# Local attention in a four-layer stream: softmax weights divided ahead of their transposes, values as the stationary operand

## Chip, cores and metric

One of the cores of a Trainium2 chip runs the whole program. The metric is the device time of one execution in microseconds (us), the lower the better. Engines are named as in the profile: PE is TensorE (PEld its weight loads), DVE VectorE, ACT ScalarE, POOL GpSimd, SP the engine that issues the DMAs.

## What is computed

The input is x, 4 sequences of 512 tokens by 128 features, float32. Four blocks follow each other, each added to x:

```python
x = x + attn_a(layernorm(x))      # softmax attention, 16 heads of 8
x = x + ffn(layernorm(x))         # two layers, below
x = x + attn_b(layernorm(x))      # linear attention, 16 heads of 8
x = x + ffn(layernorm(x))         # the same weights again
```

The change touches only the local attention in ffn. For each of its two layers:

```python
h = shift_token(x)                        # half of the features from the token before
q, k, v = split(h @ wqkv)                 # 8 heads of 64
q, k = l2norm(q) * qs, l2norm(k) * ks
q, k = rotary_xpos(q, k)
# windows of 64 queries; keys and values of this window and the one before
attn = softmax(where(mask, -max, 8 * q @ k.T))
x = x + (attn @ v) @ wo
h = layernorm(shift_token(x)) @ w1 + b1
x = x + (h_a * gelu(h_g)) @ w2 + b2
```

## The kernel before

A first part (until some 255 us) does attn_a for all sequences. Then comes one long stream, `stream`, in which the change lies. It works on 64 tiles of 128 tokens: 2 calls of ffn x 2 layers x 4 sequences x 4 tiles. Four tiles, one sequence in one layer, are a group; there are 16 groups. After the second layer of the first call each sequence also goes through attn_b, so 4 of the 16 groups carry that work too.

The order of work is written out by hand. `STEP` lists for each engine the stages in the order in which it does them in a step, each with a lag: stage s with lag l handles tile (step - l). Group stages (wo, center, var, w1, w2) act only at a group's last tile. `engine_plan` unrolls this. The engines then run on their own, in order, and meet by semaphores only.

One tile goes through these stages (lag in brackets):

- project (0): PE makes q, k, v in nine matmuls (L1253 to L1255), one PSUM bank each. ACT squares q and k (squares, L1462) and copies v to `V` (values, L1471). SP moves the values' halves to `VS` by two DMAs (L1148), so that each window finds its keys' values over 128 partitions.
- rope (0): DVE makes the rotation out of PSUM, four multiplications (L1615, L1619) and a reduction of the squares (L1626). POOL adds the two products (L1182) and scales by the norm (L1187), which ACT makes (norm, L1511).
- turn (1): PE transposes q and k (L1264, 8 transposes), ACT copies them to `QT` and `KT` (L1482, L1486).
- scores (1): PE adds the mask by matmuls (L1277) and multiplies queries and keys (L1292) into two banks, one for each half j of the heads. soften (1): DVE takes the maxima (L1651), ACT the exponentials into `PW` (L1496, 8 instructions).
- turn_p, turn_p_2 (2): PE transposes the weights of each half (L1302, 8 transposes). ACT copies the first half to `PT` (L1518), DVE the second (L1643).
- sums (2), last in the step: PE multiplies, with `PT` stationary and the values moving (L1313). The values have a 65th column of ones, so each result carries its denominator. DVE takes the reciprocal (L1658) and multiplies it in, to `ON` (L1662).
- turn_o (3): PE transposes `ON` (L1325, 4 transposes), ACT copies the result to `OT` (L1527).
- wo (3): PE multiplies `OT` by wo (L1350). center and var (4) are the layer norm's matmuls (L1368, L1374); DVE applies it (L1677, L1681). w1 (5) is L1381, w2 (6) is L1389. DVE adds w2's result in (L1714, L1718 in the first layer, three instructions; L1707 in the second, one).

The 8 banks of PSUM are dealt out in turn in the order of PE's plan. Each new use waits until the one eight uses before it has been read (`take` and `FREED`). So the order of PE's stages also sets which reader each stage waits for:

```python
def take(kind, i):
    x = at[kind, i]
    if x >= BANKS:
        earlier, j = order[x - BANKS]
        name, value = FREED[earlier]
```

`PW` and `PT` have four slots of one half each, `V` and `VS` four of a tile.

Of the kernel before, what the change touches and what calls it, by code (L numbers as in the profile page):

```python
# [14 lines left out]
P = 128  # L15
# [110 lines left out]
def build(nc, a, out):  # L126
    with ExitStack() as top:
# [46 lines left out]
        g.V = sb("V", [P, 4, HW, DW + 1])  # L174
# [39 lines left out]
        def weights_of_stream():  # L214

            todo = []
            for layer in range(LAYERS):
                def row(name):
                    return a[name][layer:layer + 1]

                by_head = row("L0_ffn_wo").rearrange("a (cc c j d) n -> c d (a cc) j n", cc=2, c=2, j=2)
                todo += [
                    *((g.wo[DW * c:DW * c + DW, layer, 2 * cc:2 * cc + 2, :], by_head[c, :, cc])
                      for c in range(2) for cc in range(2)),
# [85 lines left out]
def attention_a(nc, a, g):  # L310
# [69 lines left out]
    with ExitStack() as ctx:  # L380
# [38 lines left out]
        with block:  # L419
# [40 lines left out]
            def _(pool):  # L460
# [8 lines left out]
                nc.gpsimd.memset(g.V[:, :, :, DW:DW + 1], 1.0).then_inc(s("front_ones"), 1)  # L469
# [227 lines left out]
            def _(act):  # L697
                nc.scalar.preload_act_table_set(EXP_AND_LN)
                for work, i in plan:
# [83 lines left out]
                    elif work == "front":  # L783
# [7 lines left out]
                        act.wait_ge(s("front_ones"), 1)  # L791
                        nc.scalar.activation(g.V[:, i, :, 0:DW],
# [189 lines left out]
def of_first(k):  # L982
# [5 lines left out]
    "PE": [("latent", 8, of_sequence),  # L988
           ("project", 0, of_tile), ("features_b", 10, of_sequence), ("turn", 1, of_tile), ("features_a", 1, of_first), ("project_a", 2, of_first),
           ("context", 9, of_sequence),  # L990
           ("turn_o", 3, of_tile), ("project_b", 10, of_sequence), ("w1", 5, of_group), ("turn_p", 2, of_tile), ("turn_p_2", 2, of_tile),
# [3 lines left out]
           ("var_y", 10, of_sequence), ("w2", 6, of_group), ("wo", 3, of_group), ("sums", 2, of_tile), ("store", 6, of_end)],  # L995
    "ACT": [("latent", 8, of_sequence),
            ("squares", 0, of_tile), ("features_b", 10, of_sequence), ("turn", 1, of_tile), ("features_a", 1, of_first), ("values", 0, of_tile), ("turn_o", 3, of_tile),
            ("center_mlp", 4, of_group), ("center_a", 3, of_first), ("center_b", 7, of_sequence),
            ("center_y", 10, of_sequence), ("split", SEQS, of_tile), ("w1", 5, of_group), ("turn_p", 2, of_tile), ("keys_b", 8, of_sequence),
            ("norm", 0, of_tile), ("var_mlp", 4, of_group), ("var_a", 3, of_first), ("var_b", 7, of_sequence),  # L1000
            ("var_y", 10, of_sequence), ("soften", 1, of_tile), ("store", 6, of_end)],
    "DVE": [("lead", 0, of_lead), ("latent", 8, of_sequence), ("rope", 0, of_tile), ("project_a", 2, of_first), ("context", 9, of_sequence), ("project_b", 10, of_sequence),
            ("w1", 5, of_group), ("turn_p_2", 2, of_tile), ("keys_b", 8, of_sequence), ("soften", 1, of_tile),
            ("tokens_b", 9, of_sequence), ("var_mlp", 4, of_group), ("var_a", 3, of_first),
            ("var_b", 7, of_sequence), ("var_y", 10, of_sequence), ("wo", 3, of_group),
            ("w2", 6, of_group), ("sums", 2, of_tile)],
    "POOL": [("lead", 0, of_lead), ("split", SEQS, of_tile), ("scale", 0, of_tile), ("w2", 6, of_group),
             ("wo", 3, of_group), ("latent", 8, of_sequence), ("var_y", 10, of_sequence)],
    "SP": [("values", 0, of_tile), ("store", 6, of_end)],
# [31 lines left out]
def stream(nc, a, g, out):  # L1041
# [5 lines left out]
    for stage, i in engine_plan("PE"):  # L1047
# [4 lines left out]
        elif stage in ("scores", "sums", "keys_b", "tokens_b"):  # L1052
# [7 lines left out]
        elif stage[:7] == "center_":  # L1060
            order += [("center", number[stage[7:], i])]
        elif stage[:4] == "var_":
            order += [("var", number[stage[4:], i])]
        elif stage in ("turn_o", "wo", "w2", "context", "features_b", "project_b", "store", "features_a", "project_a"):
            order += [(stage, i)]
    at = {x: i for i, x in enumerate(order)}

    def bank(kind, i):
        return at[kind, i] % BANKS
# [5 lines left out]
             "scores": ("exped", lambda i: i + 1), "turn_p": (("p_copied", "p_copied_2"), lambda i: i // 2 + 1),  # L1075
             "sums": ("divided", lambda i: i + 1), "turn_o": ("o_copied", lambda i: i + 1),
# [721 lines left out]
```

## Time and profile before

| | |
|---|---|
| median of 3 runs | 1001.57 us (1001.5 to 1002.53) |
| the profiled execution | 1000.6 us, of which the span is 998.5 us |
| mean granted clock of TensorE | 0.996 of full speed |
| busy: PE, DVE, ACT, POOL | 94%, 73%, 73%, 39% |
| a plain group of the stream, and one with attn_b | 41.8 us, 54.3 us |

The span runs from the first to the last instruction on the core; the 2.1 us beside it are what the device's time has around it. A busy share is a mean over stages that differ. Durations in the rows are of single instructions, which overlap at their ends with their neighbours on the same engine; from start to start they are closer together.

### The profile page before, as it was taken

Reading aid. Unit: us, or ns where it says so; the run is one execution under the profiler, and the core shown is the slowest. Engines: PE = TensorE matmul, PEld = TensorE weight load, DVE = VectorE, ACT = ScalarE, POOL = GpSimd, SP = SyncE. Lnnn points to the kernel's source line nnn. Section 1 sums busy time; section 2 is a strip of 40 time slices with the busy share of each in tenths; the row PEclk is TensorE's granted clock in tenths of the full one; section 3 lists DMA queues with packets and bytes.
Section 4 is the critical chain, followed back from the end, with each engine's and each line's share of the span. In section 5 each row is a group of like instructions: output and inputs, shape, how many; then the busy total and the mean of one; then the engine's idle time right before and its main releaser. Section 6 shows DMA issues by size and latency. Waiting matters only on the chain.

```text
span 998.5 us, 22947 instructions
## 1 busy us (share of the span) xinstructions
PE 939.0 (94%) x8744; PEld 575.5 (58%) x8744; DVE 732.4 (73%) x1218; ACT 728.0 (73%) x1563; POOL 386.4 (39%) x272
## 2 busy tenths in 40 slices
PE   8999999999789999999999999999999999999985
PEld 4333333333566676666766566666666666766752
DVE  6887878886487777777777677777677777777741
ACT  3577777778688786877867677777778868788662
POOL 2110113123366536455443534434355454544411
PEclk9999999999999999999999999999999999999999
DMA  2210100000211101011000101000011011110100
GB/s 82 66 40 10 26 2 2 3 1 2 59 29 28 24 18 33 18 28 23 18 23 17 23 18 23 17 13 22 18 23 29 18 26 25 23 39 17 34 22 11
DMA packets 23303, 23.72 MB, mean 24 GB/s; under 512 B 8626, under 2 KB 15068, under 8 KB 23196
## 3 DMA queue, kind: packets, MB, share of 16 engines
q1 hardware_dynamic: 23196, 22.27, 9.3%
q8 instruction: 71, 1.16, 0.5%
q14 instruction: 36, 0.29, 0.1%
HBM read 6.16 MB, written 1.05 MB: 7 GB/s over the span
## 4 chain that ended last, share of the span: by engine, by line
PE 54%; DVE 10%; ACT 5%; issue 3%; POOL 1%; DVEq 0%; POOLq 0%; ACTq 0%
PE psum L1381 8%; PE psum L1350 6%; PE psum L1292 5%; PE psum L1389 4%; PE psum L1313 4%; PE psum L1302 3%; PE psum L1264 3%; PE psum L1253 3%; DVE BS L1619 3%; PE psum L1374 3%; PE psum L1255 3%; PE psum L1254 3%; DVE A L1615 3%; PE psum L1368 2%; PE psum L1277 2%
## 5 line engine op out<-in xcount | busy, mean ns | idle before, releaser
L1182 POOL TENSOR_TENSOR A<-A,BS 128x1024 f32<-128x1024 f32 x62 | 146.2, 2359 | 207.1 <-DVE BS L1619 206.9
L878 DVE TENSOR_REDUCE a_M<-psum 128x2 f32<-128x1024 f32 x128 | 155.3, 1220 | 34.0 <-PE psum L651 33.2
L1187 POOL TENSOR_TENSOR A<-A,RN 128x1024 f32<-128x1024 f32 x62 | 117.9, 1902 | 89.5 <-ACT RN L1511 86.0
L1496 ACT ACTIVATE f_PW<-psum,f_NM 128x128 f32<-128x128 f32 x512 | 138.5, 381 | 18.7 <-DVE f_NM L1651 18.7
L774 ACT ACTIVATE a_PT<-psum 128x1024 f32<-128x1024 f32 x128 | 128.8, 1020 | 23.2 <-PE psum L661 23.0
L1615 DVE TENSOR_TENSOR A<-psum,cos 128x512 f32<-128x512 f32 x124 | 84.8, 684 | 35.1 <-ACT SQ L1462 35.1
L1651 DVE TENSOR_REDUCE f_NM<-psum 128x4 f32<-128x512 f32 x128 | 82.1, 683 | 38.5 <-PE psum L1292 38.5
L1462 ACT ACTIVATE SQ<-psum 128x512 f32<-128x512 f32 x124 | 72.1, 624 | 49.4 <-PE psum L1255 46.4
L1381 PE MATMUL psum<-f_mid,w 128*128 128x512 f32 (+1 forms) x192 | 87.0, 603 | 2.7 <-DVE f_mid L1681 2.7
L1313 PEld LDWEIGHTS psum<-f_VS,f_PT 128*64 128x64 f32 x1024 | 64.5, 137 | 38.8 <-issue 38.3
L1619 DVE TENSOR_TENSOR BS<-psum,sin 128x512 f32<-128x512 f32 x124 | 84.2, 679 | 0.0
L572 PE MATMUL psum<-a_PT,a_VA 128*12 128x256 f32 x1024 | 79.6, 383 | 0.6 <-ACT a_PT L774 0.6
L1626 DVE TENSOR_REDUCE SS<-SQ 128x16 f32<-128x1024 f32 x62 | 74.8, 1207 | 0.0
L1313 PE MATMUL psum<-f_VS,f_PT 128*64 128x65 f32 x1024 | 73.5, 225 | 0.6 <-DVE f_PT L1643 0.4
L1313 PE MATMUL psum<-V,f_PT 128*64 128x65 f32 x1024 | 73.6, 225 | 0.0
L1264 PE MATMUL psum<-const,A 128*128 128x128 f32 x512 | 66.8, 274 | 5.7 <-POOL A L1187 3.7
L1264 PEld LDWEIGHTS psum<-const,A 128*128 128x128 f32 x512 | 59.6, 141 | 14.7 <-POOL A L1187 4.7
L1302 PE MATMUL psum<-const,f_PW 128*128 128x128 f32 x512 | 67.1, 273 | 1.0 <-DVE BS L1619 1.0
L1292 PE MATMUL psum<-f_KT,f_QT 64*64 64x128 f32 x2048 | 67.6, 270 | 0.4 <-ACT f_KT L1486 0.4
L1302 PEld LDWEIGHTS psum<-const,f_PW 128*128 128x128 f32 x512 | 58.5, 141 | 12.9 <-issue 12.9
L1313 PEld LDWEIGHTS psum<-V,f_PT 128*64 128x64 f32 x1024 | 64.5, 137 | 0.0
L1292 PEld LDWEIGHTS psum<-f_KT,f_QT 64*64 64x64 f32 x2048 | 61.2, 134 | 5.0 <-ACT f_KT L1486 0.9
(212 smaller groups left out, 1946.1 us busy)
## 6 DMA issues: line engine op xcount, KB each, us to landing
f_VS<-V SPq DMA_DIRECT2D x112, 130.0 KB, 2.3
raw<-L_ffn_wqkv_dram SPq DMA_DIRECT2D x2, 768.0 KB, 4.8
a_XT<-L_attn_a_x_dram SPq DMA_DIRECT2D x4, 256.0 KB, 2.9
out_dram<-f_OUT SPq DMA_DIRECT2D x4, 256.0 KB, 2.3
w<-L_ffn_w_dram SPq DMA_DIRECT2D x2, 341.0 KB
tables<-const_dram SPq DMA_DIRECT2D x1, 512.0 KB, 3.7
wo<-L_ffn_wo_dram SPq DMA_DIRECT2D x8, 64.0 KB
const<-const_dram SPq DMA_DIRECT2D x1, 264.0 KB, 3.1
```

Of the source, the lines that this page charges most:

```text
L774: nc.scalar.activation(PT[:, i % 4, :, :], psum[:, pair("by_key", i), :], ACT.Exp, scale=float(DA) ** -0.5).then_inc(s("exped"), 1)
L878: nc.vector.tensor_reduce(M[:, quads % 2, t, 2 * j:2 * j + 2], psum[:, pair("scores", i), :], AX_X, ALU.max).then_inc(s("maxed"), 1)
L1182: nc.gpsimd.tensor_tensor(A[:, k % 2, :, :], A[:, k % 2, :, :], BS[:, k % 2, :, :], ALU.add)\
L1187: nc.gpsimd.tensor_tensor(x, x, RN[:, k % 2, :, None].to_broadcast([P, 2 * HW, DW]), ALU.mult)\
L1264: last = nc.tensor.transpose(dst[:, P * c:P * c + P], A[:, k % 2, w, P * c:P * c + P], g.ident)
L1292: last = nc.tensor.matmul(dst[j][WIN * w:WIN * w + WIN, P * c:P * c + P].rearrange("p (s x) -> p s x", s=2), QT[rows, k % 2, c, WIN * w:WI ...
L1302: last = nc.tensor.transpose(dst[:, P * c:P * c + P], PW[:, u % 4, c, :], g.ident)
L1313: last = nc.tensor.matmul(dst[WIN * w:WIN * w + WIN, c, :], PT[:, u % 4, c, WIN * w:WIN * w + WIN], values[:, k % 4, 2 * c + j, :], start= ...
L1381: nc.tensor.matmul(take(kind, 3 * i + blk)[0:w, :], w1[:, layer, first + lo:first + lo + w], mid[:, :], start=True, stop=True).then_inc(s( ...
L1496: last = nc.scalar.activation(PW[:, u % 4, c, :], psum[:, bank("scores", u), P * c:P * c + P], ACT.Exp, bias=NM[:, u % 4, c:c + 1])
L1615: nc.vector.tensor_tensor(A[:, k % 2, w, :].rearrange("p (h d) -> p h d", d=DW), x.rearrange("p (h d) -> p h d", d=DW), g.cos[:, layer, t, ...
L1619: nc.vector.tensor_tensor(BS[:, k % 2, w, :].rearrange("p (h s d) -> p h s d", s=2, d=DW // 2), x.rearrange("p (h s d) -> p h s d", s=2, d ...
```

## The change

The softmax weights are divided by their sum before they are transposed, not the result after the multiplication:

- A new stage weigh, lag 2. DVE sums the exponentials of a tile over its keys (one reduction over 128 x 1024 of `PW`) and takes the reciprocal of the 8 sums. POOL multiplies `PW` by it in place.
- turn_p moves to lag 3, to the head of PE's and DVE's step. It waits for POOL's multiplication. Both copies to `PT` are DVE's, one behind the other, first in its step; ACT's is gone.
- sums moves to lag 3 on PE, from the end of the step to behind turn. The values (64 columns, no ones) are now the stationary operand and `PT` moves. The result is then already turned, features by tokens, and takes one bank for the tile, not two. ACT copies it to `OT`.
- turn_o, `ON`, the division and the column of ones go away. wo's rows stand in plain order and are loaded by one DMA a layer in place of four.
- Around it, project stands behind turn_p on PE, latent behind project. On DVE the layer norm's application and the addition of w2's result move from the end of a step to the head of the next, ahead of weigh and rope. On ACT values stands ahead of turn.

```diff
 STEP = {
+    "PE": [("turn_p", 3, of_tile), ("turn_p_2", 3, of_tile),
+           ("project", 0, of_tile), ("latent", 8, of_sequence), ("features_b", 10, of_sequence), ("turn", 1, of_tile),
+           ("sums", 3, of_tile), ("features_a", 1, of_first), ("project_a", 2, of_first), ("context", 9, of_sequence),
+           ("project_b", 10, of_sequence), ("w1", 5, of_group),
...
+           ("var_y", 10, of_sequence), ("w2", 6, of_group), ("wo", 3, of_group), ("store", 7, of_end)],
+    "ACT": [("squares", 0, of_tile), ("latent", 8, of_sequence), ("features_b", 10, of_sequence), ("values", 0, of_tile),
+            ("turn", 1, of_tile), ("sums", 3, of_tile), ("features_a", 1, of_first),
...
+    "DVE": [("lead", 0, of_lead), ("turn_p", 3, of_tile), ("var_mlp", 5, of_group), ("var_a", 4, of_first),
+            ("var_b", 8, of_sequence), ("var_y", 11, of_sequence), ("w2", 7, of_group),
+            ("weigh", 2, of_tile), ("latent", 8, of_sequence), ("rope", 0, of_tile),
+            ("project_a", 2, of_first), ("context", 9, of_sequence), ("project_b", 10, of_sequence),
+            ("w1", 5, of_group), ("keys_b", 8, of_sequence), ("soften", 1, of_tile),
+            ("tokens_b", 9, of_sequence), ("wo", 3, of_group)],
+    "POOL": [("lead", 0, of_lead), ("split", SEQS, of_tile), ("weigh", 2, of_tile), ("scale", 0, of_tile), ("w2", 6, of_group),
              ("wo", 3, of_group), ("latent", 8, of_sequence), ("var_y", 10, of_sequence)],
...
+                    elif stage == "weigh":
+                        k = i
+                        pool.wait_ge(s("den_recip"), k + 1)
+                        x = PW[:, 2 * (k % 2):2 * (k % 2) + 2, :, :].rearrange("p u c x -> p (u c) x")
+                        nc.gpsimd.tensor_tensor(x, x, RD[:, k % 2, :, None].to_broadcast([P, 2 * PAIRS, P]), ALU.mult)\
+                            .then_inc(s("weighed"), 1)
...
                 def turn_p(u):
-                    pe.wait_ge(s("exped"), u + 1)
+                    pe.wait_ge(s("weighed"), u // 2 + 1)
...
+                    dst = take("sums", k).rearrange("p (c x) -> p c x", c=PAIRS)
+                    pe.wait_ge(s("p_copied"), 2 * k + 2)
+                    for c in range(PAIRS):
+                        for w, values in ((0, VS), (1, V)):
+                            for j in range(2):
                                 last = nc.tensor.matmul(
-                                    dst[WIN * w:WIN * w + WIN, c, :], PT[:, u % 4, c, WIN * w:WIN * w + WIN],
-                                    values[:, k % 4, 2 * c + j, :], start=True, stop=True)
+                                    dst[DW * j:DW * j + DW, c, WIN * w:WIN * w + WIN],
+                                    values[:, k % 4, 2 * c + j, :],
+                                    PT[:, (2 * k + j) % 4, c, WIN * w:WIN * w + WIN], start=True, stop=True)
+                    last.then_inc(s("sums"), 1)
...
-                def turn_o(k):
...
+                    elif stage == "weigh":
+                        k = i
+                        dve.wait_ge(s("exped"), 2 * k + 2)
+                        if k >= 2:
+                            dve.wait_ge(s("weighed"), k - 1)
+                        x = PW[:, 2 * (k % 2):2 * (k % 2) + 2, :, :].rearrange("p u c x -> p (u c) x")
+                        nc.vector.tensor_reduce(RD[:, k % 2, :], x, AX_X, ALU.add).then_inc(s("den"), 1)
+                        dve.wait_ge(s("den"), k + 1)
+                        nc.vector.reciprocal(RD[:, k % 2, :], RD[:, k % 2, :]).then_inc(s("den_recip"), 1)
```

## Rows read from the trace of the kernel before

**Rows 1.** The page's first part: busy time, share, instructions of each engine.
```profile
PE 939.0 (94%) x8744; PEld 575.5 (58%) x8744; DVE 732.4 (73%) x1218; ACT 728.0 (73%) x1563; POOL 386.4 (39%) x272
```

**Rows 2.** Windows: stretch, length, busy time per engine, PEclk, DMA share, GB/s.
```profile
250.00:270.00 20.00, 14.64 (x174) 10.19 (x173) 7.80 (x15) 10.42 (x26) 7.76 (x8) 0.91 0.27 74
...
386.40:428.20 41.80, 40.74 (x420) 28.64 (x419) 32.28 (x58) 32.58 (x81) 20.69 (x14) 1.00 0.11 24
...
607.00:661.30 54.30, 51.72 (x461) 34.39 (x461) 39.70 (x74) 39.41 (x93) 23.16 (x16) 1.00 0.08 19
```

**Rows 3.** Waits of PE: us in total, times, longest us.
```profile
PE psum L1277 <- DVE BS L1619: 12.9, 20, 1.3
...
PE psum L1253 <- DVE f_mid L1677: 4.9, 4, 1.2
```

**Rows 4.** Timeline of PE, behind w1: start, length, instructions, [idle before].
```profile
455.63 1.03 PE L1264 MATMUL psum<-const,A 128*128 128x128 f32 x8
456.50 0.60 PE L1325 MATMUL psum<-const,f_ON 128*128 128x128 f32 x4
456.94 1.04 PE L1302 MATMUL psum<-const,f_PW 128*128 128x128 f32 x8
458.61 0.41 PE L1277 MATMUL psum<-constb 64*64 64x512 bf16 x4 [0.64 <-DVE BS L1619]
...
459.82 2.85 PE L1389 MATMUL psum<-f_hidden,w 128*128 128x512 f32 x6
462.60 0.27 PE L1313 MATMUL psum<-f_VS,f_PT 128*64 128x65 f32 x1
...
463.68 0.50 PE L1253 MATMUL psum<-f_qkv_h,HH 128*128 128x512 f32 x1
...
465.87 1.03 PE L1264 MATMUL psum<-const,A 128*128 128x128 f32 x8
```

**Rows 5.** Groups by line and shape: busy us, mean ns, idle before.
```profile
L1187 POOL TENSOR_TENSOR A<-A,RN 128x1024 f32<-128x1024 f32 x62 | 117.9, 1902 | 89.5 <-ACT RN L1511 86.0
...
L1626 DVE TENSOR_REDUCE SS<-SQ 128x16 f32<-128x1024 f32 x62 | 74.8, 1207 | 0.0
...
L1313 PE MATMUL psum<-f_VS,f_PT 128*64 128x65 f32 x1024 | 73.5, 225 | 0.6 <-DVE f_PT L1643 0.4 <-issue 0.2
...
L1662 DVE TENSOR_TENSOR f_ON<-psum,f_RD 128x256 f32<-128x256 f32 x128 | 54.3, 424 | 4.6 <-DVE f_RD L1658 0.2
...
L1643 DVE COPY f_PT<-psum 128x512 f32<-128x512 f32 x64 | 43.6, 682 | 4.0 <-PE psum L1302 2.1
...
L1658 DVE RECIPROCAL f_RD<-psum 128x4 f32<-128x4 f32 x128 | 22.1, 173 | 0.0
```

**Rows 6.** Instructions of L1681: min, median, max ns, starts.
```profile
L1681 DVE TENSOR_SCALAR f_mid<-f_mid,vecs x16: 485/487/985, 317.3 to 982.6; 128x512 f32<-128x512 f32 x16
```

**Rows 7.** Timeline of ACT behind w1.
```profile
453.22 2.17 ACT L1496 ACTIVATE f_PW<-psum,f_NM 128x128 f32<-128x128 f32 x8 [0.34 <-DVE f_NM L1651]
455.23 1.14 ACT L1462 ACTIVATE SQ<-psum 128x512 f32<-128x512 f32 x2
...
456.75 0.59 ACT L1486 ACTIVATE f_KT<-psum 128x512 f32<-128x512 f32 x1
```

**Rows 8.** Timeline of DVE, behind w1 and behind w2.
```profile
452.49 1.29 DVE L1651 TENSOR_REDUCE f_NM<-psum 128x4 f32<-128x512 f32 x2 [0.56 <-PE psum L1292]
...
455.98 0.69 DVE L1615 TENSOR_TENSOR A<-psum,cos 128x512 f32<-128x512 f32 x1 [1.10 <-ACT SQ L1462]
...
462.70 1.53 DVE L1714 SCALAR_TENSOR_TENSOR HH<-psum,vecs,Y 64x512 fp32r<-64x512 f32 x2 [1.32 <-PE psum L1389]
464.27 0.75 DVE L1718 SCALAR_TENSOR_TENSOR Y<-psum,vecs,Y 128x512 f32<-128x512 f32 x1
```

**Rows 9.** Timeline of POOL behind w1.
```profile
452.96 1.90 POOL L1187 TENSOR_TENSOR A<-A,RN 128x1024 f32<-128x1024 f32 x1 [3.50 <-ACT RN L1511]
```

More of the change, by code:

```diff
@@ L219, in row @@
                     return a[name][layer:layer + 1]
-                by_head = row("L0_ffn_wo").rearrange("a (cc c j d) n -> c d (a cc) j n", cc=2, c=2, j=2)
                 todo += [
-                    *((g.wo[DW * c:DW * c + DW, layer, 2 * cc:2 * cc + 2, :], by_head[c, :, cc])
-                      for c in range(2) for cc in range(2)),
+                    (g.wo[:, layer, :, :], row("L0_ffn_wo").rearrange("a (c p) n -> p (a c) n", p=P)),
                     (g.w1[:, layer, :], row("L0_ffn_w1").rearrange("a p n -> (a p) n")),
@@ L1000 @@
             ("norm", 0, of_tile), ("var_mlp", 4, of_group), ("var_a", 3, of_first), ("var_b", 7, of_sequence),
[L1001 to L1006, printed above, removed]
@@ L1051, in stream @@
             order += [("turned_q", i), ("turned_k", i)]
-        elif stage in ("scores", "sums", "keys_b", "tokens_b"):
+        elif stage in ("scores", "keys_b", "tokens_b"):
             order += [(stage, 2 * i), (stage, 2 * i + 1)]
@@ L1063, in stream @@
             order += [("var", number[stage[4:], i])]
-        elif stage in ("turn_o", "wo", "w2", "context", "features_b", "project_b", "store", "features_a", "project_a"):
+        elif stage in ("sums", "wo", "w2", "context", "features_b", "project_b", "store", "features_a", "project_a"):
             order += [(stage, i)]
@@ L1074, in stream @@
              "turned_q": ("qk_copied", lambda i: 2 * i + 1), "turned_k": ("qk_copied", lambda i: 2 * i + 2),
-             "scores": ("exped", lambda i: i + 1), "turn_p": (("p_copied", "p_copied_2"), lambda i: i // 2 + 1),
-             "sums": ("divided", lambda i: i + 1), "turn_o": ("o_copied", lambda i: i + 1),
+             "scores": ("exped", lambda i: i + 1), "turn_p": ("p_copied", lambda i: i + 1),
+             "sums": ("o_copied", lambda i: i + 1),
              "wo": ("y_mid", lambda i: i + 1), "center": ("ln_used", lambda i: i + 1),
@@ L1146, in _ @@
                         if k >= 4:
-                            sp.wait_ge(s("sums"), 2 * k - 6)
+                            sp.wait_ge(s("sums"), k - 3)
                         sp.dma_start(VS[WIN:P, k % 4, :, :], V[0:WIN, k % 4, :, :]).then_inc(s(f"moved{k % 4}"), 16)
@@ L1231, in take @@
                         name, value = FREED[earlier]
-                        if earlier == "turn_p":
-                            name = name[j % 2]
                         pe.wait_ge(s(name), value(j))
@@ L1342, in _ @@
                         sums(i)
-                    elif stage == "turn_o":
-                        turn_o(i)
                     elif stage == "wo":
@@ L1512, in _ @@
                           .then_inc(s("norm"), 1)
[L1513 to L1521 removed]
+                    elif stage == "sums":
                         k = i
                         m, t = k // TILES, k % TILES
[L1524 removed]
+                        act.wait_ge(s("sums"), k + 1)
                         if m >= 1:
@@ L1527, in _ @@
                         nc.scalar.activation(OT[:, :, P * t:P * t + P],
-                                             psum[:, bank("turn_o", k), :].rearrange("p (c x) -> p c x", c=PAIRS),
+                                             psum[:, bank("sums", k), :].rearrange("p (c x) -> p c x", c=PAIRS),
                                              ACT.Copy).then_inc(s("o_copied"), 1)
```

81 lines of the change are left out of this document (17 added, 64 removed).

## The prediction

> **What bounds the kernel now.** I read the busy shares first. PE is busy for 94% of the span, DVE for 73%, ACT for 73%, POOL for 39% [rows 1]. The page says that a busy PE is modelled, so the share alone proves nothing. Next came the windows of one group each. A plain group of four tiles (12 of the 16) takes 41.8 us, and PE is busy for 40.74 of them. A group with the work of attention b takes 54.3, PE 51.72 [rows 2]. In both DVE has room: 32.28 of 41.8, 39.70 of 54.3. Third, the waits of PE: the largest, over the whole span, is 12.9 us, in 20 waits, the mask matmul L1277 for a bank that the rotation on DVE (L1619) still reads [rows 3]. So in the stream TensorE's own issue rate sets the time, at a granted clock of 1.00, the 2.4 GHz level. A microsecond taken from PE there is a microsecond of the kernel, until another engine's chain becomes longer than PE's step.
>
> A rule of the Trainium skill speaks against this reading. "Perfetto Trace Analysis", section Identifying the Most-Contended Engine, says that matmul busy time is no measure of how near TensorE is to its roofline, and that the busy share of LDWEIGHTS is. That share is 58% here [rows 1], and 28.64 of 41.8 us in a plain group [rows 2]. Taken as the judge of what bounds, it would leave PE idle a third of the time. By that rule the removed transposes would come out of idle time, and the sum would be 0; by the rows, in which PE starts stage after stage with 0.64 us of waiting in a step [rows 4], it is what follows. I go by the rows and keep the other as a rival.
>
> **Part 1, PE: turn_o goes.** The four transposes of turn_o start at 456.50 and the next stage at 456.94: 0.44 us for a tile [rows 4]. 64 tiles x 0.44 = 28.2 us. Their records sum to more than that, since neighbours overlap; the distance from start to start is the price.
>
> **Part 2, PE: values stationary.** sums keeps its count of matmuls; the weights stay 128 x 64, the moving operand goes from 65 columns to 64. One tile's sums take 463.68 - 462.60 = 1.08 us, for 32 records of 225 ns [rows 4, 5], that is, they run two by two, on either half of the columns. In the old order consecutive matmuls went to output rows 0 to 63 and 64 to 127, by w; in the new order they do so by j. I take the overlap as kept. The gain is 1/65 of 1.08, 0.017 us, x 64 = 1.1 us. If the pairs no longer overlap, 32 records cost twice as much: 1.08 us more per tile, 69 us. That is one of the cases below, and the far bound.
>
> **Part 3, DVE.** It loses two reciprocals and two multiplications a tile: 2 x (173 + 424) = 1.19 us. It gains the second copy (682 ns), a reduction over 128 x 1024 in SBUF, whose nearest row is L1626 with the same shape (1207 ns), and one reciprocal of 8 columns, nearest the 173 ns of 4 columns [rows 5]. Added 2.06, net 0.87 us a tile, 3.5 a group: 35.8 us of DVE in a plain group, 43.2 in one with attention b. DVE stays below PE, but at nine tenths of a plain group of about 40 us. The reduction has bounds of 0.68 (half as wide, if it were like the maximum over 512 of rows 8) and 1.5 us; the upper one would add 0.3 x 4 = 1.2 us of DVE to a group.
>
> **Part 4, POOL and ACT.** POOL gets one multiplication of 128 x 1024 by a broadcast for each tile, nearest L1187 with 1902 ns [rows 5]: 7.6 us a group. The window's POOL time goes from 20.69 [rows 2] to 28.3 of 40, no bound. ACT loses its copy of the turned half and keeps the one of turn_o under another name. Neither costs anything by itself, because PE's 40 us cover both. The Trainium skill ("SBUF — State Buffer", in the part on reading the engine diagram) says that VectorE in a two-port mode and GpSimd lock each other out of a shared port for a whole instruction. By a lock held through one of POOL's 1.90 us instructions, each of the 16 L1681 would come up to 1.9 us late, 30 us in all if PE waited for each; the row that bears on it shows a median of 487 ns and a largest of 985 [rows 6], so 0.5 us at most so far, and w1 comes some 3 us behind it in PE's new order. I take nothing for it.
>
> **Part 5, waits: PE's own order.** The bank order changes with the stages. A step has ten banks, not twelve, and the mask matmuls now take the banks of turn_p, which the two first copies free early. The 12.9 us at L1277 go [rows 3]. What is late next, step by step:
>
> *The step behind w1.* Let M be the start of the maxima, 452.49 [rows 8]; PE is then 0.15 past its scores. PE goes on with turn_p 0.87 (456.50 - 455.63), project 2.19 (465.87 - 463.68), turn 0.87, sums 1.08, mask 0.2 [rows 4], and wants the keys at M + 5.1. ACT starts the squares at 455.23, M + 2.74, behind the exponentials, and moves on by (456.75 - 455.23) / 3 = 0.51 an instruction [rows 7]. The values now stand ahead of the turned queries and keys, so the key copy is the fifth and not the fourth: it starts at M + 4.8 and lands at M + 5.4. PE waits about 0.3 us. On DVE, weigh waits for the exponentials (until 455.39, M + 2.9 [rows 7]) and ends at M + 4.4; queued behind it is the rotation, which starts 1 us later than its 455.98 = M + 3.5 [rows 8]. It lasts 2.6 us (455.98 to the end of the wait at 458.61 [rows 4, 8]), and POOL adds and scales behind it. The next turn is 3.1 us behind the end of w2, that is covered.
>
> *The step behind w2.* Let W be w2's end, 462.60 [rows 4]. DVE first copies the two halves, until W + 1.8, then does w2's three instructions, 2.3 us (462.70 to 465.02 [rows 8]), then weigh, 1.4: the rotation starts at W + 5.5 and frees the bank of q at W + 6.8. wo takes that bank, and PE is there at W + 0.87 + 2.19 + 0.87 + 1.08 + 1.2 = W + 6.2. That is 0.6 us, and only for groups of the first layer (8 of 16), since the last layer has one instruction: 0.3 on average.
>
> *The step behind the variance matmul.* The bank of v is now freed by DVE's use of the centred values, which stands behind both copies. The same pair of waits, L1253 for L1677, took 1.2 us at worst [rows 3]; PE does turn_p and two thirds of project before it comes there, so I take 0.2.
>
> Together 0.8 us a group, 16 x 0.8 = 12.8 us. Bounds are 0 and, with each at 0.5 us more, 37.
>
> In the groups with attention b, two more instructions of DVE stand ahead of the rotation and the keys' bank waits for it, now behind copies and weigh too: 0.7 us x 4 = 2.8 us, between 0 and four times 2.
>
> **Part 6, fill and drain.** turn_p and sums of a tile move one step back, 0.87 + 1.08 = 1.95 us of PE work, from the steps of the fill, where PE was already idle for 5.36 of 20 us [rows 2], to the end. I take 2 us; bounds 0 and one plain step, 10. Moved along on ACT, DVE and SP are the later lags; SP's two transfers of values per tile keep their place, and their wait, for the sums of the tile four back, is met in the step before.
>
> **Sum.** 28.2 + 1.1 + 12.9 - 12.8 - 2.8 - 2 = 24.6 us. The profiled execution took 1000.6 us for a span of 998.5, so 976.0. It lies 0.97 us under the median of the runs, so I predict 977.0 us against 1001.57, 2.5% faster.
>
> **Rivals.**
> 1. *DVE becomes the bound (slower).* In a plain group DVE idles 41.8 - 32.28 = 9.5 us today [rows 2], much of it because its order is fixed. Its work rises to 35.8. Break-even is where it must still idle 6.0 us a group; my forecast leaves it about 4.2. For it: the rotation sits behind copies, w2 or the layer norm, and weigh, all in one queue, and everything on PE one step later hangs on the rotation. Against: most of the present idle time ends with PE's own results. If 6.5 us of idle remain, a group takes 42.3, 16 x 0.5 = 8 us: 1010 us.
> 2. *POOL makes turn late.* Behind w1 the scaling ran from 452.96 to 454.86 [rows 9] and turn started at 455.63 [rows 4], 0.77 us of slack. PE's way from w1's end to turn shrinks by 1.1 us (sums gone from it) while ACT, rid of one copy, is 0.5 earlier: 0.2 us of slack are left. With weigh ahead of it in POOL's queue and running longer than 1.9 us, turn waits 0.5 us in every step: 64 x 0.5 less the 0.2 hidden, some 19 us, 996 us.
> 3. *The new waits don't come* because PE's stages are spaced widely enough elsewhere: without the 12.8 and 2.8 us, 961 us.
> 4. *The matmul pairs stop overlapping:* 977 + 69 = 1046 us. Against it: the halves of the output alternate as before.
> 5. *PE was not the bound,* as its weight loads' share would have it: no change, 1001 us. Against it the waits of rows 3.
>
> **How the numbers follow.** The forecast's own case (966 to 990) gets 0.60, rival 1 0.14, rival 2 0.10, rival 3 0.10, rival 4 0.02, rival 5 0.04. Faster are the forecast, rival 3 and most of rival 2: 0.79. Within 0.2%, which is about what a measurement of this kernel can tell from no change: 0.06, rival 5 and the edge of rival 2. Slower: 0.15. The range from 958 to 1003 leaves out rival 4, the greater part of rival 1, and little on the low side.
>
> **What would show it.** Right, if no L1325 group is left and a plain group's window is near 40.0 us; if PE's waits for DVE at the mask are gone and short ones stand at scores (for the key copy), at wo (for the sine) and at project (for L1677); if sums still take 1.08 us a tile; if DVE's time in that window is near 35.8. Wrong, if DVE is busy all through a group; if turn waits for POOL's scaling in most steps; or if the records of sums start one by one, 57 ns or more apart.

## The result, and the profile after

The changed kernel takes 1020.57 us (median of 4 runs, 1020.0 to 1021.04) against 1001.54 us for the kernel before in the same series: ratio 1.0188, 95% interval 1.0171 to 1.0206. It is 19 us slower. The forecast was 977.0, in a range from 958 to 1003. Its profiled execution has a span of 1017.5 us.

The page's first part, of the kernel after:

```profile
PE 928.1 (91%) x8488; PEld 552.1 (54%) x8488; DVE 786.4 (77%) x1154; ACT 701.0 (69%) x1499; POOL 506.1 (50%) x335
```

PE has 256 matmuls fewer and 10.9 us less of busy time than in [rows 1], yet the span is 19 us longer: PE idles more, 89 us in place of 60. Where it does, the windows say. Of the kernel after: a stretch of the fill, the plain group that answers to the one in [rows 2], a group with attention b, and two slices of that group:

```profile
290.00:310.00 20.00, 16.80 (x183) 12.60 (x181) 12.98 (x20) 13.54 (x36) 11.34 (x8) 0.85 0.12 28
...
367.60:407.60 40.00, 39.22 (x405) 26.74 (x403) 35.63 (x55) 30.79 (x78) 28.23 (x18) 1.00 0.11 25
...
599.20:660.90 61.70, 52.76 (x446) 33.35 (x445) 42.56 (x70) 37.95 (x90) 30.72 (x20) 0.97 0.07 16
...
615.00:618.00 3.00, 1.45 (x2) 0.30 (x2) 1.50 (x2) 0.00 (x0) 2.15 (x1) 0.81 0.00 0
618.00:620.00 2.00, 2.00 (x33) 1.53 (x36) 0.00 (x0) 1.31 (x4) 0.16 (x1) 0.50 0.00 0
```

A plain group went from 41.8 to 39.9 us (from one first w1 matmul to the next, 367.66 to 407.62 to 447.51), as forecast. A group with attention b went from 54.3 to 61.7. In it DVE is busy for 42.56 of 61.7 us, less of the time than in a plain group (35.63 of 40.0), so over such a group as a whole DVE isn't full. In one stretch of it DVE is, as its timeline below shows. In the last window the granted clock is 0.50, TensorE's level of 1.2 GHz, just behind a stretch in which PE idled.

The first w1 matmul of each group is a milestone that both traces have. The distances between them split the 19 us. In the chain of the kernel after, five of them:

```profile
327.75 5.35 PE psum L1367 x12
...
367.66 5.35 PE psum L1367 x12
...
599.21 5.15 PE psum L1367 x12
...
660.91 5.15 PE psum L1367 x12
...
775.82 5.35 PE psum L1367 x12
```

| stretch between first w1 matmuls | before | after | difference |
|---|---|---|---|
| start to the first | 319.75 | 327.75 | +8.0 |
| next four (plain) | 167.19 | 159.65 | -7.5 |
| next five (the work of attention b) | 259.74 | 288.42 | +28.7 |
| next five (plain) | 208.21 | 197.82 | -10.4 |
| rest of the span | 43.61 | 43.86 | +0.2 |

Three of the five stretches in the third row are whole groups with attention b: 54.3 us each before, 61.7 after. Its first and last steps reach into the groups beside them: 49.0 went to 50.2, and 47.9 to 53.2.

What PE waits for in the kernel after, whole span: us in total, times, longest us.

```profile
PE psum L1253 <- DVE Y L1665: 13.4, 9, 2.3
PE psum L1354 <- DVE X L1751: 11.9, 4, 3.0
PE psum L1253 <- DVE f_mid L1653: 11.2, 14, 2.6
PE psum L1302 <- POOL f_PW L1189: 7.0, 3, 3.2
```

The waits of [rows 3] at the mask are gone. In their place PE waits at project (L1253) for a bank that the layer norm on DVE frees (L1665, L1653; the second was 4.9 us before), at center_y (L1354) for DVE's addition of project_b's result (L1751), and in the fill at turn_p (L1302) for POOL's weigh (L1189).

The worst step of a group with attention b, in PE's timeline of the kernel after (start, length, instructions, idle before):

```profile
612.46 1.13 PE L1430 MATMUL psum<-f_OF,wo_b 128*128 128x512 f32 x2
616.55 1.79 PE L1354 MATMUL psum<-X,const 128*128 128x512 f32 x2 [2.97 <-DVE X L1751]
618.28 0.64 PE L1277 MATMUL psum<-constb 64*64 64x512 bf16 x4
618.71 1.81 PE L1292 MATMUL psum<-f_KT,f_QT 64*64 64x128 f32 x32
...
628.01 0.50 PE L1253 MATMUL psum<-w_h,HH 128*128 128x512 f32 x1 [2.28 <-DVE Y L1665]
```

DVE in the same stretch:

```profile
606.63 1.29 DVE L1629 TENSOR_REDUCE f_NM<-psum 128x4 f32<-128x512 f32 x2 [1.49 <-PE psum L1292]
...
609.72 1.28 DVE L1621 COPY f_PT<-psum 128x512 f32<-128x512 f32 x2
610.91 1.21 DVE L1638 TENSOR_REDUCE f_RD<-f_PW 128x8 f32<-128x1024 f32 x1
...
614.64 1.21 DVE L1604 TENSOR_REDUCE SS<-SQ 128x16 f32<-128x1024 f32 x1
615.76 0.74 DVE L1751 SCALAR_TENSOR_TENSOR X<-psum,bo_b,X 128x512 f32<-128x512 f32 x1
...
624.63 1.29 DVE L1621 COPY f_PT<-psum 128x512 f32<-128x512 f32 x2 [2.74 <-PE psum L1302]
625.84 1.40 DVE L1662 TENSOR_TENSOR HH<-psum,f_LR 64x512 fp32r<-64x512 f32 x2
627.27 0.69 DVE L1665 TENSOR_TENSOR Y<-psum,f_LR 128x512 f32<-128x512 f32 x1
```

Two things can be read in DVE's queue here. DVE works without a gap from the maxima at 606.63 to the end of the addition L1751 at 616.50. From 609.72 the two copies, weigh, the rotation and its reduction stand ahead of the addition L1751, though project_b's result was there at 613.6; PE waits until 616.5. So this wait hangs on the amount of DVE's work behind the maxima, and not on idle time in the queue. Later DVE idles 2.74 us in front of a copy that waits for PE's turn_p, while the layer norm queued behind it (its LR was ready on ACT at 622.97) could have run; PE, two stages later, waits 2.28 us for that norm's bank. And the scores at 618.71 take 1.81 us, in place of 1.04, at the lower clock.

### The profile page after: what moved, and what is told of

Same layout as the page of the kernel before. It is cut to its first block, busy times and chain, and to the rows that moved or that the text cites. A ratio compares the mean times of both kernels' runs of the same rounds, so it can differ in the third digit from the quotient of the medians.

```text
span 1017.5 us, 22172 instructions
## 1 busy us (share of the span) xinstructions
PE 928.1 (91%) x8488; PEld 552.1 (54%) x8488; DVE 786.4 (77%) x1154; ACT 701.0 (69%) x1499; POOL 506.1 (50%) x335
## 4 chain that ended last, share of the span: by engine, by line
PE 49%; DVE 14%; issue 5%; ACT 4%; POOL 3%; DVEq 0%; POOLq 0%; ACTq 0%
PE psum L1367 9%; PE psum L1336 5%; PE psum L1292 4%; PE psum L1312 4%; PE psum L1375 4%; PE psum L1264 3%; PE psum L1302 3%; DVE f_PT L1621 3%; PE psum L1253 3%; PE psum L1354 3%; PE psum L1255 2%; PE psum L1254 2%; PE psum L1360 2%; DVE f_RD L1638 2%; DVE BS L1597 2%
## 5 line engine op out<-in xcount | busy, mean ns | idle before, releaser
L1189 POOL TENSOR_TENSOR f_PW<-f_PW,f_RD 128x1024 f32<-128x1024 f32 x64 | 121.4, 1897 | 99.3 <-DVE f_RD L1640 97.5
L1183 POOL TENSOR_TENSOR A<-A,RN 128x1024 f32<-128x1024 f32 x62 | 118.1, 1905 | 78.1 <-ACT RN L1497 72.1
L1621 DVE COPY f_PT<-psum 128x512 f32<-128x512 f32 x128 | 82.3, 683 | 27.8 <-PE psum L1302 27.7
L1638 DVE TENSOR_REDUCE f_RD<-f_PW 128x8 f32<-128x1024 f32 x64 | 77.6, 1213 | 14.1 <-ACT f_PW L1482 13.9
L1593 DVE TENSOR_TENSOR A<-psum,cos 128x512 f32<-128x512 f32 x124 | 82.7, 667 | 0.2 <-issue 0.2
L1302 PEld LDWEIGHTS psum<-const,f_PW 128*128 128x128 f32 x512 | 59.3, 143 | 34.0 <-issue 24.3
L1302 PE MATMUL psum<-const,f_PW 128*128 128x128 f32 x512 | 68.8, 278 | 7.0 <-POOL f_PW L1189 7.0
L1264 PE MATMUL psum<-const,A 128*128 128x128 f32 x512 | 67.3, 275 | 6.7 <-POOL A L1183 4.7
L1292 PE MATMUL psum<-f_KT,f_QT 64*64 64x128 f32 x2048 | 70.4, 278 | 2.2 <-ACT f_KT L1472 1.7
L1312 PE MATMUL psum<-f_PT,f_VS 128*64 128x64 f32 x1024 | 66.3, 228 | 4.4 <-DVE f_PT L1621 2.7
L1292 PEld LDWEIGHTS psum<-f_KT,f_QT 64*64 64x64 f32 x2048 | 62.1, 138 | 10.4 <-ACT f_KT L1472 6.2
```

The source lines that it names most:

```text
L1183: nc.gpsimd.tensor_tensor(x, x, RN[:, k % 2, :, None].to_broadcast([P, 2 * HW, DW]), ALU.mult)\
L1189: nc.gpsimd.tensor_tensor(x, x, RD[:, k % 2, :, None].to_broadcast([P, 2 * PAIRS, P]), ALU.mult)\
L1264: last = nc.tensor.transpose(dst[:, P * c:P * c + P], A[:, k % 2, w, P * c:P * c + P], g.ident)
L1292: last = nc.tensor.matmul(dst[j][WIN * w:WIN * w + WIN, P * c:P * c + P].rearrange("p (s x) -> p s x", s=2), QT[rows, k % 2, c, WIN * w:WI ...
L1302: last = nc.tensor.transpose(dst[:, P * c:P * c + P], PW[:, u % 4, c, :], g.ident)
L1312: last = nc.tensor.matmul(dst[DW * j:DW * j + DW, c, WIN * w:WIN * w + WIN], values[:, k % 4, 2 * c + j, :], PT[:, (2 * k + j) % 4, c, WIN ...
```

## The experiments

Two theories. **A, order:** the loss is in what stands ahead of what in DVE's and POOL's queues. **B, load:** it is DVE's added work (the prediction's rival 1). Times are medians; each ratio is to runs of the kernel before on the same chip.

**1. norms_first.** DVE's layer norms and w2 ahead of the copies.

```diff
-    "DVE": [lead, turn_p, var_mlp, var_a, var_b, var_y, w2, weigh, ...
+    "DVE": [lead, var_mlp, var_a, var_b, var_y, w2, turn_p, weigh, ...
```

> The changed kernel with one reordering on DVE: the layer norm's applications (var stages) and the addition of w2's result stand ahead of the two copies of the turned halves, not behind them. Theory A (order: PE waits at project for a bank that DVE's layer norm frees, and the norm is queued behind copies that themselves wait for PE): the waits of L1253 for the layer norm, 13.4 and 11.2 us in the whole span, shrink to under 5 us in all; time 995 to 1003 us. Rival B (DVE's added load of 3.5 us a group is the cause): the load is the same, so the waits move elsewhere and the time stays within 4 us of 1020.6.

1001.28 us, ratio 1.0004 (0.9986 to 1.0021). One move in one list, with every instruction kept, gives back all of the 19 us. The waits for L1665 are gone, and those for L1653 fell from 11.2 to 7.0 us, not to under 5 as expected. The wait for L1751 stays as it was (PE's waits of this run):

```profile
PE psum L1354 <- DVE X L1751: 11.9, 4, 3.0
PE psum L1253 <- DVE f_mid L1653: 7.0, 5, 1.4
PE psum L1302 <- POOL f_PW L1189: 6.3, 2, 3.2
```

Its windows of a plain group and of one with attention b:

```profile
366.40:405.70 39.30, 39.13 (x405) 26.65 (x403) 35.33 (x55) 30.67 (x78) 28.20 (x17) 1.00 0.11 25
591.10:648.80 57.70, 52.29 (x445) 33.69 (x444) 42.69 (x70) 37.70 (x90) 30.79 (x19) 0.97 0.07 17
```

The plain group loses another 0.6 us (PE idles 0.17 of 39.30), the one with attention b 4.0. DVE's busy time, 35.33 us, is within 0.3 of the changed kernel's, so B's load alone does not explain the 19 us.

**2. pool_weigh_first.** POOL's weigh ahead of split.

```diff
-    "POOL": [lead, split, weigh, scale, ...
+    "POOL": [lead, weigh, split, scale, ...
```

> The changed kernel with one reordering on POOL: weigh stands ahead of split, the subtraction that prepares the second layer's projection weights in the first three steps. Theory A (the 8 us that the first group loses come from the softmax weights being queued behind split, which waits for ACT): the two waits of L1302 for POOL in the fill, 3.2 us each, go, the first w1 matmul starts at 321 to 324 us in place of 327.75, time 1014 to 1017 us. Rival (the fill loses because the added step is longer and PE's clock is at its lower level for part of it, whatever POOL's order): w1 starts within 1 us of 327.75.

1018.2 us, ratio 1.0170 (1.0155 to 1.0185). That is 1.8 us under the changed kernel by the ratios, whose intervals overlap, and outside the expected 1014 to 1017. The two waits of L1302 go, but turn's waits for POOL's scaling, now behind split, grow from 4.7 to 8.9 us. The first w1 matmul starts at 326.36, 1.4 us earlier, and not between 321 and 324 as expected: POOL's order is a part of the fill's 8 us, and this move only shifts which product is queued behind split.

**3. project_b_early.** DVE's addition of project_b's result ahead of the rotation.

```diff
-    weigh, latent, rope, project_a, context, project_b, w1, ...
+    weigh, project_b, latent, rope, project_a, context, w1, ...
```

> The changed kernel with one reordering on DVE: the addition of project_b's result (L1751) stands ahead of the rotation, not behind it. Theory A: center_y's wait for it falls from 3.0 us to about 1 in each of the 4 groups with attention b, and the following stages run at the full clock (scores 1.04 us and not 1.81): 3 to 4 us a group, time 1005 to 1010 us. Rival B (DVE's load): the same load, time within 4 us of 1020.6. A third possibility is that the rotation, now 1.3 us later, makes turn wait for POOL; then less than 2 us a group is gained.

1018.81 us, ratio 1.0186 (1.0147 to 1.0225): no difference from the changed kernel that can be told, a miss for theory A as I had put it, and within the 4 us of 1020.6 that B had expected. PE's timeline at center_y, and its waits, say why:

```profile
619.01 1.10 PE L1354 MATMUL psum<-X,const 128*128 128x512 f32 x2 [2.13 <-DVE BS L1597]
```

The releaser is now the rotation. The bank that center_y takes is one that the rotation reads, and the rotation now starts 2.0 us later behind weigh, 1.27 of them DVE's wait for project_b and 0.7 the addition itself. So center_y waits for both, and the thing that is late is the run of DVE work from the maxima on, not one instruction's place in it.

The wait is still 0.8 us shorter, and what a group makes of that hangs on the clock. Windows of two groups with attention b in this execution:

```profile
538.40:602.50 64.10, 55.97 (x446) 35.86 (x445) 42.59 (x70) 38.07 (x90) 30.74 (x20) 0.92 0.07 15
602.50:661.80 59.30, 51.19 (x445) 32.57 (x445) 42.68 (x70) 38.06 (x90) 30.73 (x20) 1.00 0.07 17
```

The changed kernel has 61.7 us in both places, at 0.97. At a granted clock of 1.00 the group is 2.4 us shorter than that, at 0.92 it is 2.4 longer.

**4. filler.** Three needless matmuls on PE while it waits for center_y.

```diff
+    dst = take("center", number[use, j])
+    for _ in range(3):
+        nc.tensor.matmul(dst, cst("center"), w1[:, 0, 0:T], start=True, stop=True)
     pe.wait_ge(s("x_new"), j + 1)
```

> The changed kernel with three more matmuls (the center matrix by 512 columns of w1, their result overwritten) on PE ahead of center_y, in the stretch in which PE waits 3 us for DVE. They are work that nothing needs, about 0.86 us each. Theory A says that the wait costs twice: once itself and once in the lower clock behind it. With the filler PE is busy through the wait, the scores behind it take 1.04 us and not 1.81, and the group gains about 1.7 us: time 1013 to 1016 us. If the clock's fall has another cause or no price, the time is 1020.6 or higher.

1019.58 us, ratio 1.0190 (1.0173 to 1.0207). No gain. The scores behind the filler did run at the full clock, 1.04 us for 1.81. But the lower clock then came behind the next wait. Windows of this run:

```profile
618.00:620.00 2.00, 2.00 (x38) 1.27 (x38) 0.33 (x1) 1.31 (x4) 0.13 (x1) 1.00 0.04 8
...
624.00:628.00 4.00, 1.72 (x7) 1.09 (x7) 3.94 (x7) 0.69 (x2) 0.89 (x1) 0.94 0.00 0
628.00:640.00 12.00, 12.00 (x101) 7.81 (x101) 6.69 (x11) 7.69 (x19) 7.76 (x6) 0.88 0.11 24
```

So in this group filling one wait kept the clock for the work just behind it, and the price came at the next wait, the one for the layer norm (L1665 in the changed kernel) at 625 to 627.

**5. act_copies_half.** The first turned half copied by ACT again, at the head of its step.

```diff
+    "ACT": [turn_p, squares, latent, ...
...
-    for u in (2 * i, 2 * i + 1):      # DVE's copies
+    for u in (2 * i + 1,):
```

> The changed kernel with ACT copying the first turned half, at the head of its step, and DVE only the second, as in the kernel before: one copy of 0.6 us a tile, 2.4 us a group, goes from DVE to ACT, the orders are otherwise the same. Rival B (DVE's load is the cause): most of the loss against the kernel before comes back, 1003 us or less. Theory A (order: DVE's layer norm stands behind a copy that waits for PE's turn_p): the second half is still turned only 0.9 us into the step, so the norm comes some 0.3 us earlier and center_y's wait shrinks by 0.6: 1008 to 1016 us.

1024.75 us, ratio 1.0222 (1.0193 to 1.0251), 4 us slower than the changed kernel, although DVE is rid of 2.4 us a group. A plain group of this run:

```profile
371.40:411.50 40.10, 39.15 (x403) 26.67 (x403) 33.19 (x50) 32.23 (x82) 28.04 (x18) 1.00 0.11 25
```

DVE's busy time fell from 35.63 to 33.19 us and the group grew from 39.9 to 40.1, since the squares, the values and the key copy are queued on ACT behind the added copy (PE waits 6.9 us in all for the key copy, 1.7 before). So in the plain groups DVE's load is not what costs, and B's 1003 us or less is missed by far. It does not speak against B everywhere. Split at the same milestones as the table above, the profiled execution is 3.4 us longer than the changed kernel's up to the first w1 matmul and 4.4 behind the last milestone, but 2.8 shorter over the five stretches with the work of attention b, and the wait for L1751 fell from 11.9 to 9.5 us. My range for A, 1008 to 1016, was missed as well: I had overlooked ACT's queue.

**6. both_orders.** Experiments 1 and 2 together.

> The changed kernel with the two reorderings that helped, together: DVE's layer norms and w2 ahead of the copies (1001.3 us alone) and POOL's weigh ahead of split (2.4 us alone). If they are independent losses, 1020.6 - 19.3 - 2.4 = 999 us, 997 to 1001.

994.92 us, ratio 0.9921 (0.9895 to 0.9948): faster than the kernel before, and 2 us under the lower end of what was expected. Together they gain more than the sum of what each gave alone, 4 us by the medians and some 6 by the ratios (0.9921, where the two gains added make 0.9986, beyond the interval). So the two do not simply add up. Against norms_first's profiled execution, 3.1 us of the 6.4 that this one's is shorter lie ahead of the first w1 matmul. Behind the one near 912 us it is 4.9 shorter, where norms_first shows granted clocks of 0.97, 0.93 and 0.86 and this run 1.00, 1.00 and 0.94; in between it is 1.5 longer. What set the clock apart there was not tested.

**7. both_center_y_late.** As 6, with PE's center_y behind scores.

```diff
-    ("center_y", 10, ...), ("keys_b", 8, ...), ("tokens_b", 9, ...), ("scores", 1, ...),
+    ("keys_b", 8, ...), ("tokens_b", 9, ...), ("scores", 1, ...), ("center_y", 10, ...),
```

> both_orders with PE's center_y behind scores, not ahead of keys_b and scores. Theory: in a group with attention b, PE comes to center_y 3 us before both things it needs, the addition of project_b's result and a bank that the rotation reads, since DVE works without a gap from the maxima through the division of tokens_b, the copies, weigh and the rotation. Doing mask and scores (1.2 us) in that time gains 1 to 2 us in each of 4 groups: 4 to 8 us under both_orders, 991 to 996. If the scores need the same bank and so wait as long, it is within 2 us of both_orders.

990.93 us, ratio 0.9879 (0.9841 to 0.9917), 4 us under both_orders, with intervals that overlap. A group with attention b takes 55.7 us (57.7 in both_orders), at a granted clock of 1.00. PE's waits for L1751 fall from 11.9 to 1.6 us in all; 5.1 us stand new at the mask, for the rotation:

```profile
586.30:642.00 55.70, 50.87 (x446) 32.74 (x445) 42.69 (x70) 37.78 (x90) 30.79 (x19) 1.00 0.08 18
```

**8. both_act_copies.** As 6, with the ACT copy of 5.

> both_orders with the first turned half copied by ACT at the head of its step. In the groups with attention b DVE's unbroken run from the maxima to project_b's addition is 0.6 us shorter and center_y's wait falls from 3.0 to 2.4; in plain groups DVE isn't the last to finish before anything and nothing changes, unless the copy, queued on ACT behind the exponentials, is late for sums. 2 to 4 us under both_orders, 995 to 998; if DVE's load binds in the plain groups as well, 985 to 990; if the copy is late for sums, above both_orders.

998.1 us, ratio 0.9954 (0.9930 to 0.9978), 3 us slower than both_orders and not 2 to 4 faster as expected first; the intervals overlap slightly. The wait for L1751 fell from 11.9 to 9.5 us in all, as expected, and the waits for the key copy grew to 7.1 us; plain groups take 39.8 us in place of 39.3, the three whole groups with attention b 57.1, 55.5 and 57.1 in place of 57.7. Here too the load taken from DVE is worth something in attention b, and ACT's queue costs more elsewhere.

**9 and 10. dve_more_at_end, dve_more_at_head.** One more DVE instruction a tile, of 0.68 us, in two places.

```diff
+    nc.vector.tensor_reduce(spare[:, :], w1[:, 0, 0:T].rearrange("p (c x) -> p c x", c=4), AX_X, ALU.max)
```

at_end it stands behind soften's two maxima, at_head behind the two copies.

> The changed kernel with one more DVE instruction a tile, a maximum over 128 x 512 of a constant that nobody reads (0.68 us), behind the maxima of soften, where DVE has idle time: 2.7 us a group, 43 us over the span. Rival B (DVE's load binds): a plain group grows from 39.9 to 41 us or more, time 1040 us or more. Theory A (only what stands ahead of the layer norm, the rotation and project_b in DVE's queue costs): plain groups stay within 0.3 us of 39.9; in the groups with attention b it delays the division of tokens_b and with it the whole run behind, up to 1 us each: 1021 to 1027 us.

> The same added instruction, 0.68 us a tile, one behind each copy of the turned halves is two a tile, so 1.36 us a tile ahead of the layer norms, weigh and the rotation. Theory A: PE's waits for the layer norm's bank and for project_b's addition each grow by about 1.2 us; a plain group goes from 39.9 to 41 to 43, one with attention b from 61.7 to 65 or more: 1045 to 1080 us, that is, at least four times the price of the same instruction at the end, for twice the load. Rival B (load alone): twice the effect of the run beside it.

1035.75 us, ratio 1.0357 (1.0310 to 1.0405), and 1058.42 us, ratio 1.0581 (1.0553 to 1.0609). The second expectation speaks of two instructions a tile; the kernel that ran has one, like the first, as DVE's busy time shows. So the pair compares the same load in two places. A plain group's window of dve_more_at_end:

```profile
374.30:414.60 40.30, 39.18 (x403) 26.72 (x404) 37.76 (x58) 30.82 (x77) 28.23 (x18) 1.00 0.11 25
```

And of dve_more_at_head:

```profile
370.40:411.60 41.20, 39.23 (x405) 26.77 (x403) 37.87 (x59) 30.87 (x76) 28.25 (x18) 1.00 0.10 24
```

From w1 to w1 these are 40.2 and 41.1 us, against 39.9 without it. The same instruction costs 0.3 us a group behind the maxima and 1.2 ahead of the norm, weigh and rotation. By the ratios it costs 17 us of the whole time at the end and 39 at the head, a factor of 2.3, where load alone would cost the same in both places. At neither is it free.

at_end misses its range (1021 to 1027). Its profiled execution took 1046.5 us, the longest of the four, and was 27 us longer in span than the changed kernel's: 16 of them lie in the five stretches with the work of attention b, whose three whole groups take 66.6, 62.9 and 67.3 us at granted clocks of 0.90, 0.97 and 0.90, and 6 lie ahead of the first w1 matmul.

**11. both_weigh_behind_rope.** As 6, with DVE's weigh behind the rotation.

> both_orders (994.9 us) with DVE's weigh behind the rotation, not ahead of it. The rotation, its reduction and in the attention b groups project_b's bank come 1.4 us earlier, so center_y's wait for the bank goes, while project_b's addition stays as late as before, since weigh is still ahead of it. On POOL weigh still comes first and waits for DVE's reciprocal, so add and scale start later, by the rotation's length: turn may wait for them in each step. If PE's slack there covers it: 990 to 995 us; if not, 16 to 64 waits of 0.5 to 1.5 us: 1005 to 1040. I expect the second.

1066.13 us, ratio 1.0648 (1.0625 to 1.0671), beyond the expected 1040. A plain group takes 44.5 us. The waits of PE:

```profile
PE psum L1302 <- POOL f_PW L1189: 32.8, 25, 4.1
PE psum L1264 <- POOL A L1183: 32.3, 26, 3.3
```

POOL takes weigh first; if its input comes behind the rotation, POOL's sum and scaling are late for turn and the weights late for turn_p. So weigh's place ahead of the rotation is right, for all that it costs in attention b.

**12. best.** The norms first, center_y late, and POOL's split last.

```diff
-    "POOL": [lead, split, weigh, scale, ...
+    "POOL": [lead, weigh, scale, split, ...
```

> DVE's layer norms and w2 ahead of the copies, POOL's split last in its step (behind weigh and scale), PE's center_y behind scores. Against both_center_y_late (990.9 us) only split's place differs: turn no longer waits for a scaling that is queued behind split in the fill (2.5 and 1.8 us), unless the second layer's projection then waits for the split weights, which it needs first at the 17th tile. 984 to 989 us.

991.51 us, ratio 0.9890 (0.9869 to 0.9912), 1.1% faster than the kernel before, above the expected 984 to 989 and not told apart from both_center_y_late. The first w1 matmul starts at 319.44 (319.75 before the change), so the fill's loss is gone. In the profiled execution part of that went again elsewhere, as these two of its windows show, both groups with attention b:

```profile
525.70:585.90 60.20, 55.38 (x445) 34.57 (x445) 42.86 (x71) 37.86 (x90) 30.89 (x20) 0.91 0.07 16
585.90:641.50 55.60, 50.78 (x445) 32.66 (x445) 42.10 (x69) 37.71 (x90) 30.68 (x19) 1.00 0.08 18
```

## Why the prediction was wrong

**Right.** PE's issue sets the pace of the plain groups, and removed matmuls come off the time: forecast 40.0 us a group, measured 39.9. That it fits to 0.1 us is in part luck: PE's busy time fell by 1.5 us a group and not 1.8, and its idle time by 0.3, where I had let new waits take the place of the old ones in full. The sizes held: weigh's reduction 1213 ns (1207 taken) and its reciprocal 203 (173 taken), POOL's multiplication 1897 (1902 taken), DVE 35.63 us a plain group (35.8), POOL 28.23 (28.3). sums still takes 1.08 us a tile, so the pairs overlap, against rival 4. Rival 5, that PE doesn't bind because its weight loads are busy for 58% only, falls with the plain groups. Taking nothing for delays at L1681 (now L1657) was right for the time: they sum to some 2 us, as before. But the median of 487 ns hides that they come, as the last section shows. Rival 2 didn't come: turn waits for POOL's scaling (L1183) 4 times in the span, 4.7 us in all. The mask's waits went; the waits at project for the norm's bank are there, 0.3 us in a plain group (0.2 taken), and the wait for the key copy, 0.3 us a group in the forecast, is recorded 3 times in the whole span, 1.7 us in all.

**The step that failed** is the term for the groups with attention b in part 5, "0.7 us x 4 = 2.8 us, between 0 and four times 2". With the removed work counted in, such a group should have gone from 54.3 to some 53. It went to 61.7. Over the five stretches of the table the removed work was to take 9 us from 259.7 and this term to add 2.8; 288.4 were measured, so that in place of 2.8 us stand some 38, far beyond the term's bound of 8. In the group from 599.2 to 660.9 PE's recorded waits are 3.3 us for L1665, 3.0 for L1751, 1.7 for L1653 and 0.8 for the rotation, 8.8 in all, against 2.6 in the answering group before. PE's busy time is 52.76 us, where 51.73 less four times 0.44 would be 50.0. Of these 2.8 us some 2 are matmuls drawn out at the clock's lower level: groups with attention b that ran at 1.00 have 50.8 (both_center_y_late) to 51.2 us (project_b_early) of PE's busy time. 6.2 and 2.8, less 1.8 for the removed work, are 7.2 of the 7.4 us. I had written out three steps of the plain group and given the fourth kind one sentence, looking only at the keys' bank. That DVE's norms in attention b stand behind two copies, which wait for PE's turn_p, was to be read in the list, and so was that both the addition and the bank of center_y stand behind the rotation. The prediction also took no price for the clock at all.

**The second failed term** is fill and drain, 2 us (bounds 0 and 10). The drain cost 0.2, the fill 8.0. I hadn't seen POOL's split ahead of weigh, which holds turn_p back twice by 3.2 us, and PE's clock, at 0.85 in the window from 290 to 310, falls behind such waits. Experiment 12 brings the start of w1 back to 319.44; how much of the 8 us is the clock alone was not separated.

**Rival 1** had the right sign, and in its argument DVE's queue, but it put the loss into the plain groups: 42.3 us, measured 39.9. DVE's load over a group is not the cause, since DVE's order alone gives back 19 us (1) and added work costs by where it stands (9, 10). One wait does go with the load: the one for L1751, behind DVE's unbroken run from the maxima. It stays at 11.9 us in all when the norms are moved (1), falls to 9.5 when one copy of 0.68 us goes from the run (5, 8) and grows to 14.3 with 0.68 us more in it (10). Rival 3's plain group, 39.2 us, came about only after the reordering of experiment 1, with 39.3.

What stays open: both_center_y_late and best still need 55.6 to 55.7 us for a group with attention b, where 54.3 less 1.8 would be 52.5. Waits of 1.4 us for L1653, 1.3 for the rotation at the mask, 0.8 and 0.7 are in their traces; no run took these away.

## What to carry to other kernels

When work moves between engines in a hand-written order, the sum of the durations is the easy half; write the timetable for every kind of step, the rare ones first, since their queues are the longest. In an in-order queue, look at what an instruction that waits has behind it: here a copy that waited for PE held a layer norm whose input was ready, and PE's next stage waited for that norm's bank. If a change loses, try the orders before giving up on it: the same instructions ran in 1020.6 us and, with three entries moved, in 991.5.

## What the runs showed of the hardware

The same waits can cost very different amounts. In one execution of best, two groups with the same instructions and the same waits recorded on PE (1.4, 1.3, 0.8, 0.7 and 0.4 us) took 60.2 us at a mean granted clock of 0.91 and 55.6 at 1.00. Within the first, the clock read 0.77 over 540 to 546, in which PE was busy for 3.62 of 6 us, and 0.66 in the 6 us behind it; in the second the answering stretch, with 3.63 of 6 busy, kept 1.00. So how long PE idled in such a stretch does not alone decide whether the clock goes to its lower level. The scatter of whole runs goes with the clock: the four runs of dve_more_at_end range from 1031.8 us at a mean of 0.983 to 1046.5 at 0.962, those of the changed kernel, with waits as long, from 1020.0 to 1021.0 at 0.983 and 0.984. Why one kernel scatters and the other does not was not tested.

A DVE instruction can also be held up by one on POOL. L1657, a scaling of 128x512 in SBUF, ran 16 times in the changed kernel. In 7 of these POOL was in the middle of an instruction when it began, and the 7 took 650 to 960 ns; each ended 0.28 or 0.29 us behind POOL's instruction. The other 9 took 480 to 490 ns. One of the 7, and POOL beside it:

```profile
484.46 0.96 DVE L1657 TENSOR_SCALAR f_mid<-f_mid,vecs 128x512 f32<-128x512 f32 x1
...
483.23 1.91 POOL L1183 TENSOR_TENSOR A<-A,RN 128x1024 f32<-128x1024 f32 x1
```

In the kernel before it was 4 of 16, at 0.98 us each. So in these rows the delay follows what is left of POOL's instruction: at most 0.5 us, since none of the L1657 began early in one.

The Trainium skill ("TensorE: Matmul & The Clock Gate", section HAM oscillation — how this bites in real kernels) describes waits that send TensorE back to its lower clock, so that the work behind them starts slow. The trace agrees: 0.50 from 618 to 620 us, behind the wait for L1751, and 1.81 us for scores that take 1.04. What one pays is not fixed by the wait, as the two groups of best show, and a wait that is filled can leave the price to the next one (experiment 4).
